# Context maxima of attention's first item computed during the projections, its loads two batches after the start, and the second item's load issued at once

## What is computed

```python
def _L0_xattn_ref(x, cross_input, ...):          # H = 16 heads of D = 16
    q, k, v = (_heads(x @ W + b) for W, b in ((Wq, bq), (Wk, bk), (Wv, bv)))
    att = where(causal, einsum('bhqd,bhkd->bhqk', q, k) * scale, -inf)
    y = einsum('bhqk,bhkd->bhqd', softmax(att, axis=-1), v)
    qc = _heads(x @ Wcq + bcq)
    kc, vc = _heads(cross_input @ Wck + bck), _heads(cross_input @ Wcv + bcv)
    attc = einsum('bhqd,bhkd->bhqk', qc, kc) * scale          # 1601 context keys
    y = y + einsum('bhqk,bhkd->bhqd', softmax(attc, axis=-1), vc)
    return y.transpose(0, 2, 1, 3).reshape(...) @ Wp + bp
x = x + tanh(g_xattn[0]) * _L0_xattn_ref(_layernorm(x), ctx_512, ...)
x = x + tanh(g_ffn[0]) * _L0_ffn_ref(_layernorm(x), ...)      # routed experts, two layers
```

## Time and profile before

| | |
|---|---|
| median of 3 runs | 2816.75 us (2814.58 to 2819.35) |
| the profiled execution's own time | 2810.69 us |
| its span in the profile | 2808.6 us |
| TensorE busy, mean granted clock | 2489.5 us, 0.94 |
| VectorE, ScalarE, GpSimd busy | 1931.8, 1576.7, 478.8 us |
| DMA, MB over the span | 305.70 MB, mean 109 GB/s |
| projections: first output on VectorE to last | 26.7 to 237.75 us |
| attention: first context maximum, first score | 242.3, 279.8 us |

### The profile page before, as it was taken

The page is one execution under the profiler, slowest core; times in us unless marked ns, Lnnn a source line. Parts: engine busy times, 40 slices in busy tenths (PEclk is TensorE's granted clock), DMA queues, the critical chain, the costliest instruction groups (busy, mean ns, idle before and its releaser), DMA issues. The chain is left out here.

```text
span 2808.6 us, 55075 instructions
## 1 busy us (share of the span) xinstructions
PE 2489.5 (89%) x20166; PEld 1507.6 (54%) x20166; DVE 1931.8 (69%) x3187; ACT 1576.7 (56%) x3345; POOL 478.8 (17%) x541
## 2 busy tenths in 40 slices
PE   7886999999999999999999998767599968969896
PEld 6773444444444444444444444666487857857675
DVE  8776888888888888888888882544234534634546
ACT  4440777777777777777777776322144423423432
POOL 2002000101010100000010102222303141340413
PEclk9996999999999999999999998768799989989998
DMA  7999757565665647475655623311234312321433
GB/s 267 400 359 237 96 81 104 77 90 75 91 83 85 88 71 104 70 105 67 92 82 85 81 40 90 129 63 57 75 92 120 92 68 61 110 90 35 147 98 98
DMA packets 164962, 305.70 MB, mean 109 GB/s; under 512 B 45607, under 2 KB 112334, under 8 KB 156366
## 3 DMA queue, kind: packets, MB, share of 16 engines
q1 hardware_dynamic: 151358, 265.56, 45.4%
q0 software_dynamic: 12288, 33.57, 3.8%
q10 hardware_dynamic: 1072, 3.23, 0.5%
HBM read 165.13 MB, written 127.68 MB: 104 GB/s over the span
## 5 line engine op out<-in xcount | busy, mean ns | idle before, releaser
L804 ACT ACTIVATE at_P<-at_ST 128x512 f32<-128x512 f32 (+4 forms) x2176 | 1095.9, 559 | 371.8 <-PE at_ST L847 349.5
L755 DVE TENSOR_REDUCE f_part<-at_R 128x2 f32<-128x804 f32 x1024 | 976.0, 994 | 121.1 <-PE at_R L835 117.1
L862 PE MATMUL at_OP<-at_P,at_V 128*32 128x256 f32 x8192 | 641.4, 385 | 16.0 <-ACT at_O L812 12.9
L847 PE MATMUL at_ST<-at_Q,at_K 64*128 64x512 f32 (+4 forms) x1428 | 343.9, 455 | 3.5 <-ACT at_P L804 3.5
L862 PEld LDWEIGHTS at_OP<-at_P,at_V 128*32 128x32 f32 x8192 | 163.1, 108 | 264.0 <-ACT at_P L804 186.7
L835 PE MATMUL at_R<-at_K,at_Q 64*128 64x402 f32 x1344 | 271.0, 392 | 5.1 <-DVE f_part L755 5.1
L738 POOL TENSOR_SCALAR_AFFINE_SELECT at_P<-at_P 128x512 f32<-128x512 f32 x128 | 81.6, 637 | 1088.8 <-ACT at_P L804 1088.8
L847 PEld LDWEIGHTS at_ST<-at_Q,at_K 64*128 64x128 f32 (+1 forms) x1428 | 141.7, 180 | 218.5 <-ACT at_P L804 203.6
L752 DVE TENSOR_REDUCE f_mx<-at_R 128x2 f32<-128x256 f32 (+3 forms) x256 | 209.9, 821 | 42.7 <-PE at_R L828 40.7
L1757 DVE TENSOR_TENSOR ex_ab<-ex_bank,ex_sg 128x256 f32<-128x256 f32 x148 | 62.8, 424 | 239.8 <-ACT ex_sg L1840 182.1
L1700 POOL DMA_INDIRECT ex_gb<-expert_rows,c_IDX x128 | 126.0, 984 | 430.3 <-DMA expert_rows<-ex_rb 314.1
(11 more groups left out here) (240 smaller groups left out, 4242.6 us busy)
## 6 DMA issues: line engine op xcount, KB each, us to landing
at_K<-k_parts SPq DMA_DIRECT2D x126, 264.1 KB, 9.1
k_parts<-pj_kpart SPq DMA_DIRECT2D x32, 800.5 KB, 9.5
ex_xb<-sorted SPq DMA_DIRECT2D x148, 128.0 KB
expert_rows<-ex_rb SPq DMA_DIRECT2D x148, 128.0 KB
v_items<-pj_vbuf SPq DMA_DIRECT2D x32, 544.0 KB, 9.5
q_parts<-pj_qpart SPq DMA_DIRECT2D x32, 512.0 KB, 11.0
at_Q<-q_parts SPq DMA_DIRECT2D x252, 64.0 KB, 9.8
f_K<-k_parts SPq DMA_DIRECT2D x60, 264.1 KB, 9.5
```

The source lines that it names most:

```text
L755: dve.tensor_reduce(part[:, :, p, q, c], buf[:, :, 0:XC], AX.X, ALU.max).then_inc(s_drain, 1)
L804: act.activation(Pt[(NKT * n + s) % NP][0:rows, h, c0:T], ST[(NST * n + s * G + h) % NB][0:rows, c0:T], ACT.Exp, scale=SCALE).then_inc(s_e ...
L847: pe.matmul(ST[t % NB][0:rows, c0:T], K[n % NU][half, p, keys], Q[n % NU][half, kind, p, c0:T], start=True, stop=True).then_inc(s_st, 1)
L862: ins = pe.matmul(OP[32 * h:32 * h + 2 * D, at], V[n % 2][0:rows, key_tile(s), h, :], Pt[(NKT * n + s) % NP][0:rows, h, at], start=s in (0 ...
```

## The change

1. The 32 context `MAX` tiles of item 0 and their combination leave attention. `First.max_tile` (TensorE) and `First.take` (VectorE) do them in batches 4 to 7, 8 a batch: before every third output (k = 2, 5, ..., 20) and one after the last. They use a single PSUM tile R of two banks, so tile m waits until tile m - 1 has been reduced.
2. For R, NBANK falls from 6 to 4.
3. Item 0's loads are issued in batches 2 and 3, not 6 and 7. ScalarE loops over batches 0 and 1, has 2 and 3 written out, loops over 4 to 6, has 7 written out.
4. TensorE and VectorE loop over batches 0 to 3 and have 4 to 7 written out.
5. In attention SyncE issues `load(1)` before it waits for the writes; GpSimd does `ones(1)` before that wait, the V memsets after it. The order of everything behind is the same: `load_values(1)`, then the shift copies of item 0.

```diff
@@ class First
+    def max_tile(self, pe, m, buf):
+        p, q, c = XTILES[m]
+        if m == 0:
+            pe.wait_ge(self.s_ld, 16 * LOADS)
+        else:
+            pe.wait_ge(self.s_took, m)
+        for h in range(2):
+            half = slice(64 * h, 64 * h + 64)
+            ins = pe.matmul(buf[:, h, 0:XC], self.Q[half, 1, p, q * P:(q + 1) * P],
+                            self.K[half, p, T + XOFF[c]:T + XOFF[c] + XC], start=True, stop=True)
+        ins.then_inc(self.s_max, 1)
+
+    def take(self, dve, m, buf):
+        p, q, c = XTILES[m]
+        dve.wait_ge(self.s_max, m + 1)
+        dve.tensor_reduce(self.part[:, :, p, q, c], buf[:, :, 0:XC], AX.X, ALU.max).then_inc(self.s_took, 1)
+        if m == len(XTILES) - 1:
+            dve.wait_ge(self.s_took, m + 1)
+            dve.tensor_reduce(self.mx[:, 1].rearrange("p h r q -> p (h r q)"),
...
@@ stage_project
-        NBANK = 6
+        NBANK = 4
...
+        R = r_.ps("R", [P, 2, T])
+        BL, BM = 2, B - 4
+        NMB = len(XTILES) // (B - BM)
@@ VectorE; TensorE has the same with first.max_tile
-                def body(b, more):
+                def body(b, more, tiles=()):
+                    tiles = list(tiles)
                     for k, o in enumerate(outs):
                         bank = acc[k % NBANK]
+                        if k % 3 == 2 and tiles:
+                            first.take(dve, tiles.pop(0), R)
...
+                    for m in tiles:
+                        first.take(dve, m, R)
...
-                with dve.Fori(0, B - 1) as b:
+                with dve.Fori(0, BM) as b:
                     body(b, True)
-                body(B - 1, False)
+                for b in range(BM, B):
+                    body(b, b + 1 < B, range(NMB * (b - BM), NMB * (b - BM + 1)))
@@ ScalarE
-                with act.Fori(0, B - 2) as b:
+                with act.Fori(0, BL) as b:
                     body(b, True)
-                body(B - 2, True, 0)
-                body(B - 1, False, 1)
+                for h in range(2):
+                    body(BL + h, True, h)
                 first.load_values(act, VS)
                 const.gates(act)
+                with act.Fori(BL + 2, B - 1) as b:
+                    body(b, True)
+                body(B - 1, False)
@@ stage_attend
-        events = [("MAX", 0, m) for m in range(NMX)] + [("SHIFT", 0, CROSS)]
+        events = [("SHIFT", 0, CROSS)]
...
+                load(1)
                 for n in WRITES:
                     sp.wait_ge(first.s_wr[n], written(n, B))
-                load(1)
                 load_values(1)
                 shift_rows(0, CROSS)
@@ GpSimd
-                for n in WRITES:
-                    pool.wait_ge(first.s_wr[n], written(n, B))
-                for u in range(2):
-                    pool.memset(V[u][:, :, :, D:2 * D], 1.0).then_inc(s_one, 1)
...
                 ones(1)
+                for n in WRITES:
+                    pool.wait_ge(first.s_wr[n], written(n, B))
+                for u in range(2):
+                    pool.memset(V[u][:, :, :, D:2 * D], 1.0).then_inc(s_one, 1)
+                pool.wait_ge(s_one, 4)
                 values(0)
```

More of the change, by code:

```diff
@@ L44 @@
 NKE = NK + NK % 2
+XC = 402
+XOFF = [0, 400, 800, TC - XC]
+XTILES = [(p, q, c) for p in range(2) for q in range(QT) for c in range(4)]
+LOADS = 20
 def bcast(ap, n, axis):
@@ L160, in __init__ @@
         self.s_ld, self.s_vld, self.s_fill = r_.sem("ld0"), r_.sem("vld0"), r_.sem("fill0")
+        self.s_max, self.s_took = r_.sem("max0"), r_.sem("took0")
         self.s_wr = {n: r_.sem("wr_" + n) for n in WRITES}
@@ L186, in load_rows @@
             eng.dma_start(self.Q[rows, kind].bitcast(F32), q[0, h, kind]).then_inc(self.s_ld, 16)
+    def max_tile(self, pe, m, buf):
[16 more added lines that the diff above has]
+            dve.tensor_reduce(self.mx[:, 1].rearrange("p h r q -> p (h r q)"),
+                              self.part[:, :, :, :, :].rearrange("p h r q c -> p (h r q) c"), AX.X, ALU.max
+                              ).then_inc(self.s_took, 1)
     def load_values(self, eng, VS):
@@ L475, in transpose_x, with body @@
                         ins.then_inc(s_T, 1)
-                def body(b, more):
+                def body(b, more, tiles=()):
+                    tiles = list(tiles)
                     for k, o in enumerate(outs):
+                        if k % 3 == 2 and tiles:
+                            first.max_tile(pe, tiles.pop(0), R)
                         if k == NSELF and more:
@@ L517, in body @@
                         ins.then_inc(s_out, 1)
+                    for m in tiles:
+                        first.max_tile(pe, m, R)
                 transpose_x(0)
-                with pe.Fori(0, B - 1) as b:
+                with pe.Fori(0, BM) as b:
                     body(b, True)
-                body(B - 1, False)
+                for b in range(BM, B):
+                    body(b, b + 1 < B, range(NMB * (b - BM), NMB * (b - BM + 1)))
 def stage_attend(nc, a, QS, KS, VS, YS, XS, XR, idf, idm, mqm, first):
@@ L561, in stage_attend @@
         NST = NKT * G
[L562 to L565, removed]
+        mtiles = [("x", *m) for m in XTILES]
         NMX = len(mtiles)
@@ L641, in load @@
                         if r == 2 and n < NU:
-                            sp.wait_ge(s_one, 2 * n + 2)
+                            sp.wait_ge(s_one, 4 * n - 2)
                         for h in range(2):
@@ L705, in _ @@
             def _(pool):
-                for n in WRITES:
-                    pool.wait_ge(first.s_wr[n], written(n, B))
-                for u in range(2):
-                    pool.memset(V[u][:, :, :, D:2 * D], 1.0).then_inc(s_one, 1)
                 def ones(n):
                     for h in range(2):
-                        pool.wait_ge(s_one, 2 * n + h)
                         pool.memset(K[n][64 * h + 32:64 * h + 64, :, :].bitcast(F32), 1.0).then_inc(s_one, 1)
-                    pool.wait_ge(s_one, 2 * n + 2)
+                    pool.wait_ge(s_one, 4 * n - 2)
                 def values(n):
@@ L887, in _ @@
                     elif e[0] == "SHIFT":
-                        if e[2] == CROSS:
-                            pe.wait_ge(s_pm, n + 1)
+                        if e[2] == CROSS and n == 0:
+                            pe.wait_ge(first.s_took, NMX + 1)
+                        elif e[2] == CROSS:
+                            pe.wait_ge(s_pm, n)
                         else:
```

## The result

| | before | changed |
|---|---|---|
| median | 2816.58 us (2809.21 to 2823.23, 19 runs) | 2821.98 us (2817.03 to 2826.36, 19 runs) |
| ratio | | 1.002, 95% interval 1.0011 to 1.0028 |
| profiled execution, span | 2810.69, 2808.6 us | 2817.77, 2816.0 us |
| last output of the projections | 237.75 us | 250.17 us |
| first score of attention | 279.79 us | 284.61 us |

The account below looks back on a forecast made before the run. Bound: 29 us of lone maxima beside a load strand with 3.9 us slack, behind projections waiting for their writes. Removing 29.0 us, adding 10.6 us of projections and exposing the loads nets +1.0 us: 2818 us, range 2808 to 2829.

Parts of the forecast that it names:

- Loads of item 0: Batches 2 to 4: earlier loads delay batch 3's v writes from 137.86 to 149.3 us; batch 4's stretch then takes 20.6.
- Maxima in batches 5 and 6: Batches 5 and 6: 7.6 us of reductions each make VectorE the bound, 27.9 us a batch, ending at 225.7.
- Batch 7: End of projections: v writes land at 231.6 us, last output at 248.3 instead of 237.75, bounds 243.4 to 252.
- Four banks: Batches 0 to 3: nothing in the sum; about 1 us a batch where TensorE bounds, covered by the full DMA queue.
- The start of attention: Behind the last output: `load(1)` is bound by transfer, not issue; item 1 is loaded at 280.2 or about 279.3 us.
- The copies: Start of attention: shift copies land 1.5 us behind `load(1)` and the values, first score near 280.8 us.
- A: Start of attention: shift copies don't queue, item 1's first maximum near 278 us, gain 4 us, 2813 us; chance 0.1.
- B: Start of attention: `load(1)` goes faster, item 1 loaded near 269 us, gain 8.3 us, 2808.5 us; chance 0.1.
- C: Batches 4 to 7: TensorE's clock falls, losing 2 us four times, 8 us, 2826 us; chance 0.3.

Follow-up runs that it names:

- b_load0: The kernel before with only item 0's loads moved to batches 2 and 3; ratio 0.9996.
- b_banks4: The kernel before with only NBANK lowered from 6 to 4; ratio 1.0000.
- b_load1: The kernel before with only `load(1)` and GpSimd's `ones(1)` put ahead of the wait for the writes; ratio 1.0000.
- a_twoq: The changed kernel with `load(1)` split over two queues, rows 64 to 127 on ScalarE's; ratio 1.0004 against the kernel before.
- a_nomax: The changed kernel with item 0's 32 context maxima left out and set to zero; ratio 0.9966 against the kernel before.
- a_shiftq: The changed kernel with item 0's four shift copies issued on ScalarE's queue as soon as ready; ratio 0.9992 against the kernel before.
- a_same: The changed kernel run once more with nothing altered; ratio 1.0011 against the kernel before.
- a_best: a_twoq_split with item 0's shift copies issued ahead of item 1's values; ratio 0.9944 against the kernel before.
- a_mid: The changed kernel with item 0's shift copies on SyncE's queue ahead of the r = 2 rows of `load(1)`; ratio 0.9991 against the kernel before.
- a_twoq_split: The changed kernel with `load(1)` over two queues, 16 maxima in batches 4 to 6 and 16 behind the barrier; ratio 0.9967 against the kernel before.

## Why the prediction was right, step by step

The forecast was 2818 us, 2808 to 2829, with no difference the likeliest and slower next; measured were 2821.98 us and 1.002. Its mechanism held from the last output on, with two terms too small by 1.9 and 1.7 us; inside the batches it came out right in part by luck (steps 1 and 3).

1. *Loads of item 0.* Landing of batch 3's v writes forecast at 149.3 (146 to 150.5), measured 152.50. The 3.2 us lie outside the bounds; b_load0 alone has 151.89, so the loads cost 14.0 us there, not 11.4. It hardly carried on: first output of batch 5 at 170.82 against 169.9. The six reductions were still to come, as forecast, but the stretch took 18.3 us and not 20.6: each cost 0.90 us from start to start, and they filled waits of VectorE of 0.53 and 0.85 us. Two errors, +3.2 and -2.3, nearly cancelled, which is luck.
2. *Maxima in batches 5 and 6.* Forecast 27.9 us a batch, VectorE the bound; measured 28.03 and 28.02. Batch 7 began at 226.87, not 225.7.
3. *Batch 7.* The step expected a wait for the v writes until 231.6. This is the step that failed: there was no such wait. The writes had landed, and VectorE's own work and waits for ScalarE's copies and TensorE, 0.2 to 0.7 us at a time, set the batch. The last output came 23.3 us after the batch's first, not 22.6, at 250.17 instead of 248.3 (within 243.4 to 252): a length nearly right by another path.
4. *Four banks.* Nothing in the sum: right (b_banks4, ratio 1). The reason given, about 1 us a batch where TensorE is the bound, covered by the full queue, fits: 2.3 us over batches 0 and 1.
5. *The start of attention.* Forecast 31.0 to 31.9 us from the last output to the landing of the values; measured 32.7 (282.85). "Bound by the transfer, not by its issue" was the step that mattered. b_load1 (3.7 us from the earlier issue), a_twoq (2 to 3 us from a second queue) and a_nomax (30.3 us from first issue to the values) show it for the greater part of the strand.
6. *The copies.* Behind the values by 1.5 us in the forecast, 1.76 in the trace. The Trainium skill, "DMA: Bandwidth & Descriptors", section "Queues, rings and completion order", allows a later DMA on fewer rings to finish first. No run here shows it: in a_shiftq the copies landed ahead of the values (copied at 283.52), but they had been issued ahead of them too, 258.11 against 264.64.

The sum: +1.0 us forecast, +4.8 measured at the first score. The 3.8 between them are 1.9 from the last output, 1.7 from the strand behind it (32.7 against the 31.0 of the lower figure, which the sum took) and 0.3 from the copies. The span of the profiled execution grew by 7.4 us and that of a_same by 12.0, with first scores 4.8 and 3.7 later and ends of attention 5.7 and 3.9 later; what lies behind attention is spread between executions, and single spans say nothing of 5 us.

*Rivals.* A (copies don't queue) did not happen: 19.17 us of wait on them. B (`load(1)` faster) did not: 29.3 us from first issue to the values, against 26 before. C (clock) fell: 1.00 in batches 5 to 7, although TensorE stopped at each R. It was given 0.3 on the strength of batch 7's 0.79 before, where TensorE had stood still for the writes; the change took that long wait away, and through the many short ones the clock stayed at 1.00.

What the prediction did not see is its own remedy: it listed the copies behind `load(1)` and the values as a fact of the order, and did not ask what it would be worth to swap them. In a_best that swap is 3.2 us of first score.

What stays open: a_best's ratio (15 us, interval 11.5 to 18.8) is more than its trace shows by the end of attention (8.7 us sooner than before). What lies behind the end of attention takes 972 to 979 us in the nine traces on the 2680 us chips, so single traces can't tell where the rest comes from; the later stages were not followed. Nor was it tried whether fewer than 16 maxima ahead of the barrier are better still, or the swap alone on the changed kernel.

## What to carry to other kernels

Before work is moved out of the way of something, look for the strand that runs beside it and read where that one ends: here it was 3.9 us short of the maxima, so of 29 us removed 7.3 could be gained with that strand as it was, even had the maxima been free (a_nomax), and the price in the stage that took them was 12.1. Work that can run beside a transfer is divided so that both end together: here 16 ahead of the barrier and 16 behind it beat both 32 and 0 and 0 and 32. A small transfer that is waited for goes ahead of a large one that is not; here what counted was all that was outstanding at its issue, and not which queue it stood in (a_mid and a_shiftq: first score at 275.0 and 275.2).

## What the runs showed of the hardware

- Four copies of 4 KB took 5.5 us from their last issue to the first score behind the rows of one item, of which the last had been issued 7.5 us ahead (a_best), 8.6 with 544 KB of values more (a_twoq_split), 13.8 on a queue of their own beside the whole load (a_shiftq) and 16.3 at the end of it (after). Before the change, with the values landed, it was 3.2 us at most, as TensorE did not wait for them. A second queue did not give the copies a share of their own.
- The rows of one item, 16 partitions a transfer, go at nearly the same pace from one queue or two: 29.3 and 30.0 us from the first issue to the values against 27.0 (a_twoq). The Trainium skill, "SBUF - State Buffer", section on Door 1, would have the partitions reached as the bound; the runs agree in that a second queue brought 2 to 3 us and not half, but no run here changed the number of partitions, so they don't show that the partitions are the cause.
- TensorE's granted clock stayed at 1.00 through batches in which it was busy for 26.2 of 28.1 us and stopped every third output. It was lower in the batches in which TensorE had stood still for longer: 0.90 in batch 4 (3.70 us in one piece), 0.84 in batch 3 of the changed kernel (8.76 us), 0.79 in batch 7 before (11.92 us).
